# The output projection of the first attention in fp16 parts, with the parts made by GpSimd and the projection placed inside the third group of heads

## The reference

```python
q, k, v = einsum('bsd,hed->bhse', x, wq), ..., ...
weights = softmax(where(causal, q k^T / 8, -1e9))
heads   = weights @ v                      # 16 heads x 64
concat  = heads.transpose(...).reshape(b, s, 1024)
x       = x + concat @ wo.T                # 1024 -> 128, per token
```

## Time and profile before

| | us |
|---|---|
| median of 3 runs | 1005.44 |
| the three runs | 1005.44, 996.13, 1005.65 |
| the profiled execution | 997.58 |
| its span, first to last instruction | 995.8 |
| attention a, about | 20 to 530 of the span |

### The profile page before, as it was taken

How to read it: one execution, slowest core, us unless ns; L and a number is a source line. 1 busy time by engine, 2 the same in 40 slices (tenths; PEclk the granted TensorE clock), 3 DMA queues, 4 the chain that set the end, 5 groups by cost and what they waited for, 6 DMA issues and landing times.

```text
span 995.8 us, 25347 instructions
## 1 busy us (share of the span) xinstructions
PE 814.4 (82%) x10180; PEld 619.3 (62%) x10180; DVE 698.0 (70%) x1589; ACT 462.7 (46%) x785; POOL 409.1 (41%) x302
## 2 busy tenths in 40 slices
PE   2999999999999999999958766678777877829655
PEld 1688788887888888888845535345455445415435
DVE  4666666667666676666675775478989898867764
ACT  1667666667666676667632321222233233204220
POOL 1445444544444454444431000056767767751000
PEclk9999999999999999999988787778999999957776
DMA  6000000000000000000000000001111111110002
GB/s 258 2 3 1 0 0 0 0 0 0 0 0 0 0 0 0 0 0 0 2 1 1 1 1 1 1 3 19 21 11 21 21 14 18 22 21 1 1 1 84
DMA packets 71585, 13.16 MB, mean 13 GB/s; under 512 B 66432, under 2 KB 70528, under 8 KB 70912
## 3 DMA queue, kind: packets, MB, share of 16 engines
q1 hardware_dynamic: 71552, 12.71, 5.9%
HBM read 8.51 MB, written 4.19 MB: 13 GB/s over the span
## 4 chain that ended last, share of the span: by engine, by line
PE 56%; DVE 19%; issue 10%; ACT 10%; POOL 3%; DMA 1%; DVEq 0%; ACTq 0%; SPq 0%; POOLq 0%
PE PS L519 6%; PE PS L476 4%; PE PS L335 4%; PE PS L692 3%; PE PS L412 3%; DVE b_prod L776 3%; PE PS L337 3%; PE PS L483 3%; PE PS L336 3%; ACT a_ph L545 3%; PE PS L512 2%; PE PS L683 2%; PE PS L957 2%; PE PS L455 2%; POOL b_w L833 2%
## 5 line engine op out<-in xcount | busy, mean ns | idle before, releaser
L620 POOL TENSOR_TENSOR a_pl<-a_p,a_ph 128x1024 f16<-128x1024 f32 (+1 forms) x128 | 210.4, 1643 | 270.6 <-ACT a_ph L545 270.6
L542 ACT ACTIVATE a_p<-PS 128x1024 f32<-128x1024 f32 (+1 forms) x128 | 103.8, 811 | 89.1 <-PE PS L483 89.1
L833 POOL TENSOR_TENSOR b_w<-b_v,b_e 128x2048 f32<-128x2048 f32 x32 | 136.9, 4301 | 0.0
L587 DVE TENSOR_REDUCE a_nm<-PS 128x4 bf16<-128x512 f32 (+1 forms) x128 | 121.1, 946 | 0.4 <-PE PS L455 0.4
L576 DVE TENSOR_TENSOR a_qk_l<-PS,a_qk_h 128x512 f16<-128x512 f32 x128 | 87.9, 687 | 46.7 <-ACT a_qk_h L535 46.6
L545 ACT ACTIVATE a_ph<-PS 128x1024 f16<-128x1024 f32 (+1 forms) x128 | 102.9, 804 | 0.0
L535 ACT ACTIVATE a_qk_h<-PS 128x512 f16<-128x512 f32 x128 | 72.2, 604 | 58.0 <-PE PS L337 57.9
L683 PE MATMUL PS<-b_kh,w_rolls 128*128 128x256 f16 x256 | 68.7, 296 | 30.9 <-DVE b_prod L776 29.8
L776 DVE TENSOR_TENSOR b_prod<-PS,b_qt 128x512 f32<-128x512 f32 x128 | 84.1, 678 | 13.9 <-PE PS L685 13.7
L358 POOL TENSOR_TENSOR veps<-mv,eps 128x2 f32<-128x2 f32 (+2 forms) x40 | 7.9, 197 | 190.3 <-DVE mv L1107 139.1
L583 DVE TENSOR_TENSOR a_vl<-PS,a_vh 128x512 f16<-128x512 f32 x64 | 44.3, 692 | 54.8 <-ACT a_vh L538 54.8
(11 more groups left out here) (212 smaller groups left out, 2069.9 us busy)
## 6 DMA issues: line engine op xcount, KB each, us to landing
scratch_dram<-b_o SPq DMA_DIRECT2D x32, 64.0 KB, 4.0
b_y<-scratch_dram SPq DMA_DIRECT2D x16, 128.0 KB, 2.0
out_dram<-X SPq DMA_DIRECT2D x2, 1024.0 KB, 3.9
w_rest<-rest_dram SPq DMA_DIRECT2D x1, 1846.0 KB, 15.1
X<-x_dram SPq DMA_DIRECT2D x1, 1792.0 KB, 11.2
w_first<-first_dram SPq DMA_DIRECT2D x1, 1600.0 KB, 6.8
w_rolls<-rolls_dram SPq DMA_DIRECT2D x1, 512.0 KB, 15.3
X<-x_dram SPq DMA_DIRECT2D x1, 256.0 KB, 3.3
```

Source lines behind the costliest of these rows:

```text
L542: act.activation((a_p0, a_p1)[j][:, me, :, :, :].rearrange("p a h q -> p a (h q)"), TT[:, :, 0:512 - 256 * j], ACT.Exp, scale=EA ** -0.5)
L587: dve.tensor_reduce(a_nm[:, nx, j, :].rearrange("p (a h) -> p a h", a=2)[:, :, 0:2], MM[:, :, 0:256 * (j + 1)].rearrange("p a (h k) -> p a ...
L620: pool.tensor_tensor(*(n[:, g % 2, :, :, :].rearrange("p a h q -> p (a h q)") for n in (pl, p, ph)), ALU.subtract).then_inc(a_split, 1)
L833: pool.tensor_tensor(b_w8[:, j, :, :, :], rolled_values(par, j, 0, H), rolled_exps(par, j, 0, H), ALU.mult).then_inc(b_weighed, 1)
```

## The change

- The projection becomes three fp16 products (high x high, high x low, low x high, by `mm3`): 48 matmuls of 128 columns in place of 16 in fp32. The outputs in `a_oh` and `a_ol` and the weights in `a_wo_h` and `a_wo_l` are the high and low parts.
- Outputs keep V's factor 32 (the column of ones becomes 1.0), weights get one of 32, and the add, now with a scalar multiply in the same instruction, takes 1024 out.
- A new step `parts`, on GpSimd alone, at the end of each group: two operations over 128x512 that read `a_ot` (now double buffered, one group each) and write `a_oh` and `a_ol`. A step `weights`, once, at the end of batch 0's group 0: three operations of 128x1024 on GpSimd.
- `project` moves from the end of group 1 to group 2, between `turn` and `vlo`/`xt`. `add` is a step of its own at the end of group 2.
- New waits: ScalarE's `turn` for the parts of two groups back; TensorE's `project` for the parts; GpSimd's group 2 parts for the add; GpSimd's `weights` for the weights' load, which TensorE waited for before. The epilogue gets parts between the turns and the projection.

```diff
@@ a_steps
         put(not (first and g < 2), ("turn", 0))
+        put(g == 2 and not first, ("project", 0))
         put(prepare, ("vlo", 0))
         put(g == 1 and not last, ("norm", 0))
         put(g == 2 and not last, ("xt", 0))
@@
         put(True, ("exps", 1), ("exph", 1))
-        put(g == 1 and not first, ("project", 0))
+        put(g == 2 and not first, ("add", 0))
+        put(first and g == 0, ("weights", 0))
+        put(not (first and g < 2), ("parts", 0))
@@ epilogue
-A_EPILOGUE = [("normal", 0, 0), ("turn", 0, 0), ("pv", 0, 0), ("pv", 0, 1), ("normal", 1, 0), ("turn", 1, 0),
-              ("project", 1, 0)]
+A_EPILOGUE = [("normal", 0, 0), ("turn", 0, 0), ("pv", 0, 0), ("pv", 0, 1), ("parts", 0, 0), ("normal", 1, 0),
+              ("turn", 1, 0), ("parts", 1, 0), ("project", 2, 0), ("add", 2, 0)]
@@ TensorE
-                    if isinstance(b, int) and b == 0 and g == GA - 1:
-                        pe.wait_ge(w_loaded, 16 * 2)
@@
-                    pe.wait_ge(a_turned, GA * b)
+                    pe.wait_ge(a_parted, GA * b)
                     for t in range(QT):
+                        tok = slice(t * 128, (t + 1) * 128)
                         for c in range(8):
-                            ins = pe.matmul(dst[:, t * 128:(t + 1) * 128], a_ot[:, c, t * 128:(t + 1) * 128],
-                                            w["a_wo"][:, c, :], start=c == 0, stop=c == 7)
+                            ins = mm3(pe, dst[:, tok], a_oh[:, c, tok], a_ol[:, c, tok], a_wo_h[:, c, :], a_wo_l[:, c, :],
+                                      t == 0 and c == 0, t == 1 and c == 7)
@@ ScalarE
-                    c = 2 * ((g - 2) % GA)
-                    act.activation(a_ot[:, c:c + 2, :], src[:, :].rearrange("p (c t) -> p c t", c=2),
+                    wait(act, a_parted, u - 3)
+                    act.activation(a_ot[:, me, :, :], src[:, :].rearrange("p (c t) -> p c t", c=2),
@@ VectorE
                 elif kind == "project":
-                    dve.wait_ge(a_filled, fill.count)
+                    split[3] = R[fill.bank], fill.count
+                elif kind == "add":
+                    projected, count = split[3]
+                    dve.wait_ge(a_filled, count)
                     xb = X[:, bass.ds((b - 1) * QT, QT), :]
-                    dve.tensor_tensor(xb, R[fill.bank][:, 0:SEQ].rearrange("p (t d) -> p t d", t=QT), xb,
-                                      ALU.add).then_inc(a_added, 1)
+                    dve.scalar_tensor_tensor(xb, projected[:, 0:SEQ].rearrange("p (t d) -> p t d", t=QT),
+                                             1.0 / (V_UP * WO_UP), xb, ALU.mult, ALU.add).then_inc(a_added, 1)
@@ GpSimd
+                elif kind == "weights":
+                    pool.wait_ge(w_loaded, 16 * 2)
+                    chain.link(pool.tensor_scalar(w["a_wo"], w["a_wo"], WO_UP, None, ALU.mult))
+                    chain.link(pool.tensor_copy(a_wo_h[:, :, :], w["a_wo"]))
+                    pool.tensor_tensor(a_wo_l[:, :, :], w["a_wo"], a_wo_h[:, :, :], ALU.subtract)
+                elif kind == "parts":
+                    c = 2 * ((g - 2) % GA)
+                    pool.wait_ge(a_turned, u - 1)
+                    if g == 2:
+                        wait(pool, a_added, b)
+                    ot, oh, ol = a_ot[:, g % 2, :, :], a_oh[:, c:c + 2, :], a_ol[:, c:c + 2, :]
+                    chain.link(pool.tensor_tensor(oh, ot, zeros[:, 0:2].unsqueeze(2).to_broadcast([128, 2, SEQ]), ALU.add))
+                    pool.tensor_tensor(ol, ot, oh, ALU.subtract).then_inc(a_parted, 1)
@@ setup
-            pool.memset(a_vh[:, :, :, :, EA:W], V_UP)
+            pool.memset(a_vh[:, :, :, :, EA:W], 1.0)
```

More of the change, by code:

```diff
@@ L36 @@
 V_UP = 32.0
+WO_UP = 32.0
 CHUNKS = 2
@@ L304, in build @@
             a_o = sb("a_o", [128, 2, QT, 4, EA], stage=in_a)
-            a_ot = sb("a_ot", [128, 8, SEQ], stage=in_a)
+            a_ot = sb("a_ot", [128, 2, 2, SEQ], stage=in_a)
+            a_oh, a_ol = sb("a_oh", [128, 8, SEQ], F16, stage=in_a), sb("a_ol", [128, 8, SEQ], F16, stage=in_a)
+            a_wo_h, a_wo_l = sb("a_wo_h", [128, 8, D], F16, stage=in_a), sb("a_wo_l", [128, 8, D], F16, stage=in_a)
         b_qt = sb("b_qt", [128, 2, SEQ])
@@ L394, in build @@
         a_pv, a_normal, a_turned, a_added = sem("a_pv"), sem("a_normal"), sem("a_turned"), sem("a_added")
+        a_parted = sem("a_parted")
         def a_read(step, b):
@@ L621, in do @@
                                        ALU.subtract).then_inc(a_split, 1)
-            run_plan(pool, A_PLAN, do, chain, 1)
+                elif kind == "weights":
[11 more added lines that the diff above has]
+                    pool.tensor_tensor(ol, ot, oh, ALU.subtract).then_inc(a_parted, 1)
+            run_plan(pool, A_PLAN, do, chain, 1 + GA)
         b_filled = sem("b_filled")
```

## The result

| | us |
|---|---|
| before, median of 4 runs | 1001.64 (996.13 to 1005.65) |
| after, median of 4 runs | 1015.07 (1013.47 to 1016.88) |
| ratio, 95% interval | 1.0138 (1.0073 to 1.0204) |
| profiled execution after: time, span | 1016.88, 1015.1 |

The forecast was 1010 (999 to 1023), slower at 0.44 and no difference at 0.49. The time lies in the range and the sign is that of the forecast; but the sum made from the rows, +9.7 on the profiled execution, was half of the +19.3 between the two profiles. Three later executions (one of e1 at 1013.9, one of e9 at 1339.7, one of the kernel before at 1529.8) belong to a slower state of the chip; they are in the medians, and not in the ratios.

A forecast was written before the change was run, and what follows sets the result against it. The prediction took TensorE to bound the first attention. Its terms, 6.4 (loop) + 0.4 (last batch) + 1.5 (weights) + 1.4 (tail) = +9.7 us, on a mean of 1001.2 gave 1010.9, forecast as 1010, range 999 to 1023.

The forecast's parts named there:

- The projection's 2.65: TensorE's projection in each batch: 48 fp16 matmuls at 55 ns take 2.65 us, 1.02 less than now.
- the new stall of 1.39 for the add: Group 3's first qk on TensorE waits 1.39 us until VectorE's late add has read the projection's bank.
- group 1 to 2 at 6.53: Without the projection at group 1's end, this interval falls from 9.97 to 6.53 us, -3.44 a batch.
- 0.46 forecast: Net cost of a loop batch: -3.44 from group 1 and +3.90 in group 2, +0.46 us; fourteen batches +6.4.
- signs of being wrong: Projection over 3 us, lines 498 or 502 waiting for a_pl, waits for parts, or clock below 1.00 between 60 and 490.
- So the parts cost nothing beside this work.: GpSimd's two parts operations a group, 2.4 us, fit its 2.69 us of idle time: cost taken as 0.
- The weights: Three GpSimd operations once in batch 0, 4.3 to 6.4 us, delay what follows by 0.5 to 2.6; 1.5 taken.
- The tail: After the last turn, parts add 2.4 and the projection saves 1.0: +1.4 us; at the lower clock 2.65 more.
- Rival 1: Group 2: the projection fills a gap and nothing waits for its bank; 996 us, or 979 with a shorter projection; 8%.
- Rival 2: In the projection, matmul loads aren't hidden: 1044 us, 1027 if half exposed, 1030 at the skill's 81 ns; 6%.
- Rival 3: GpSimd becomes late in the batches by a slow broadcast add: up to 1 us a batch, +14, 1025 us; 12%.
- Rival 4: The same time: 0.3 less stall makes a batch +0.2 and the sum +5, 1006 us; 34%.

The follow-up runs named there:

- e1: Changed kernel with only the add moved, from the end of group 2 to just ahead of xt: 1004.15 us, 1.0060 of the kernel before.
- e9: Kernel before plus only GpSimd's two operations of the parts' size in every group, into tiles nobody reads: 1000.95 us, 1.0035 of the kernel before.
- e2: Changed kernel with group 1's parts made over 128x2x4 elements in place of 128x2x256: 1013.40 us, 1.0172 of the kernel before.
- e8: Changed kernel with only apply moved, from ahead of the maximum to behind vlo: 1011.30 us, 1.0139 of the kernel before.
- e4: Changed kernel with step weights moved from the end of batch 0's group 0 to the prologue's end: 1034.47 us, 1.0386 of the kernel before.
- e6: Changed kernel with project ahead of pv, add and apply behind vlo, group 1's parts earlier, weights in the prologue: 984.98 us, 0.9885 of the kernel before.
- e3: Changed kernel with the projection as the old 16 fp32 matmuls from an fp32 copy, in the same place: 1062.42 us, 1.0682 of the kernel before.

## Why the prediction was right

**Right, by their own rows.** The projection's 2.65 (2.69); the new stall of 1.39 for the add (1.40), and that the add's place and nothing else makes it (e1); group 1 to 2 at 6.53; that GpSimd keeps up (of attention a's batches, TensorE waited for a_pl in batch 0 alone). The 81 ns a matmul of the Trainium skill's page "TensorE: Matmul & The Clock Gate", section "Back-to-back issue gap", did not show: 48 took 2.69 us, 56 ns each. With ordinary batches alone the loop costs 0.67 us a batch, against 0.46 forecast. Two of the signs of being wrong came once, in the slipped batch: a projection of over 3 us (3.93), and a clock below 1.00 between 60 and 490 us (at 236.1).

**Mis-sized.** Three terms of the sum:
- "So the parts cost nothing beside this work." This is the step that failed. I asked whether GpSimd has time for its parts, and not who can't run while it works. xn met them: 0.2 to 0.3 us in an ordinary batch (the wait for a_vl grew by 0.23; e2 and e8 have 30.92 against 31.22), 3.5 in the slipped one, and 1.6 in the last batch's f_xs (8.53 for 6.90). The trace of the kernel before had a sign of it, in attention a's last batch: of the sixteen equal instructions that write f_xs, the normalized x of the feed-forward layer, at a median of 0.34 us, one took 2.14 and one 1.26 us, each beside an a_pl. The prediction made no use of it:

```profile
L363 DVE TENSOR_SCALAR f_xs<-X,mv,rstd x16: 332/338/2137, 512.6 to 519.2; 128x128 f32<-128x128 f32 x16
...
512.53 2.12 POOL L620 TENSOR_TENSOR a_pl<-a_p,a_ph 128x1024 f16<-128x1024 f32 x1
```

- The weights: 1.5 taken, 4.8 measured (e4). The three operations took 6.1 us, within my 4.3 to 6.4, though the one with a scalar (2.78) is above my bound of 2.13; and xn of batch 0 then met GpSimd (3.26 us for 0.60).
- The tail. From the end of f_xs to the last add 13.95 us for 10.84, +3.1 where +1.4 was forecast: the last projection ran largely at the lower clock level (0.50 until 550.1), in 3.95 us for 2.65, which gives 1.3 of the 1.7; the other 0.4 stays open. This was named as a possibility, at 2.65 more. Its first matmul, after the wait for the parts:

```profile
547.37 0.27 PE L341 MATMUL PS<-a_wo_h,a_oh 128*128 128x128 f16 x1 [3.12 <-POOL a_ol L643]
```

**The sum again,** profile against profile, +19.3: to xn of batch 1 +0.1 (73.83 to 73.89: the projection that left group 1 gives 3.4, the weights take 4.8, and GpSimd's first a_pl began 1.3 earlier); the 13 periods to batch 14 +12.2 (13 x 0.67 and one slip of 3.5); from there to the last add +9.3 (4.6 for the last group 2s, 1.6 for f_xs, 3.1 behind it); and the stages behind -2.3. My +9.7 had no slip (3.5), 2.8 less for xn in the loop, 3.3 less for the weights and 3.6 less for the end; the earlier start and the later stages gave 3.6 back.

**Luck.** That 1010 came within 5 us of 1015.07 is in part luck. From the profiled execution the rows gave 997.6 + 9.7 = 1007.3, and its counterpart took 1016.9. I had set out from 1001.2 instead, the mean of four executions of the kernel before (996.1, 997.6, 1005.4 and 1005.7), and that made up for terms which I had too small. In the experiments the kernel before has medians of 996.6 to 997.0; against these 1015.07 would be 1.8% slower, not 1.4%, but the changed kernel was not run beside them.

**The rivals.** Rival 1 (nothing waits behind the projection) was false here; e6 has made it true and is the faster kernel. Rival 2 was false (56 ns a matmul). Rival 3 named the right engine and the wrong mechanism: in the loop GpSimd was never late, it was in the way. Rival 4's 1006 lies below all four runs.

## What to carry to other kernels

Before giving a free engine work, ask which instructions of the other engines can't run while it works, and what is queued behind them: a wait that seems small became a slip of 2 to 5 us here as it hung on a gap of 0.1 us, and then even a gain elsewhere (e4) can leave the kernel slower. When a step moves, move with it what frees its buffer, and put it where its engine would wait anyway. Before undoing a change that lost, test its parts one at a time: here the cheaper matmuls were worth 15 to 17 us, and the order of five steps decided whether that showed.

## What the runs showed of the hardware

- VectorE's fp32 tensor_scalar from SBUF to SBUF (128x128, 0.34 us) waits for GpSimd's running tensor_tensor: its single instructions took 1.25 us beside one of 1.16 and 2.29 beside one of 2.12. VectorE's operations with an input in PSUM kept their times beside GpSimd (a_qk_l 0.686 us on the mean, 0.687 before).
- GpSimd's own times: scaling 128x1024 fp32 in place 2.78 us, more than the subtraction of two such inputs (2.13); the cast to fp16 1.04 (one instruction each).
- TensorE takes a 128-column fp16 matmul with a fresh 128x128 load every 56 ns at the upper clock level, and every 107 at the lower. After a wait of 3.08 us for a_vl its clock fell to the lower level in 8 of 23 cases (the changed kernel 1 of 1, e1 2 of 3, e4 4 of 5, e3 1 of 14).
